# Self-attention in a one-core transformer layer: scores in quarters of the array, the mask written by PE, the maximum read from PSUM

## The reference

```python
def _L0_attn_ref(x, q_heads, k_heads, v_heads, output_proj):
    ...                                   # 16 heads of 16 features
    scores = jnp.einsum('bhqd,bhkd->bhqk', q, k) * scale
    causal = jnp.triu(jnp.ones((S, S), bool), k=1)
    scores = jnp.where(causal, jnp.asarray(-jnp.inf, scores.dtype), scores)
    attn = jax.nn.softmax(scores, axis=-1)
    out = jnp.einsum('bhqk,bhkd->bhqd', attn, v)
    out = out.transpose(0, 2, 1, 3).reshape(B, S, D_MODEL)
    return out @ output_proj.T
x = x + _L0_attn_ref(_layernorm(x, axis=-1), ...)
```

## Time and profile before

| | us |
|---|---|
| median of 3 runs | 1841.96 (1841.55 to 1844.64) |
| profiled execution | 1836.55 |
| its span | 1834.8 |
| `self_attention`: first instruction on POOL to end of the last add | 1349.70 to 1442.76 |
| granted PE clock, mean of the span (1 is 2.4 GHz) | 0.964 |

### The profile page before, as it was taken

How to read it: one execution, slowest core, us unless ns; L and a number is a source line. 1 busy time by engine, 2 the same in 40 slices (tenths; PEclk the granted TensorE clock), 3 DMA queues, 4 the chain that set the end, 5 groups by cost and what they waited for, 6 DMA issues and landing times. The chain is left out here.

```text
span 1834.8 us, 31747 instructions
## 1 busy us (share of the span) xinstructions
PE 1699.0 (93%) x9178; PEld 1392.3 (76%) x9178; DVE 1488.3 (81%) x2950; ACT 1232.4 (67%) x2233; POOL 163.4 (9%) x145
## 2 busy tenths in 40 slices
PE   6599999999999999999999999998978559999994
PEld 4478888888888888888888888874544349999994
DVE  6689999899989998998999899875348558878863
ACT  4577777878777778787787777864324237777761
POOL 0000000000000000000000000000027240000003
PEclk9899999999999999999999999998989769999997
DMA  7722222222222212222223232104830066666732
GB/s 281 283 75 68 73 82 63 73 76 84 70 77 64 87 54 81 72 82 69 80 62 87 58 87 63 36 13 123 301 124 1 2 220 223 225 192 227 222 99 81
DMA packets 171170, 199.02 MB, mean 108 GB/s; under 512 B 19144, under 2 KB 131936, under 8 KB 171104
## 3 DMA queue, kind: packets, MB, share of 16 engines
q1 hardware_dynamic: 169568, 194.00, 33.4%
q0 software_dynamic: 1536, 4.20, 0.7%
HBM read 153.53 MB, written 44.63 MB: 108 GB/s over the span
## 5 line engine op out<-in xcount | busy, mean ns | idle before, releaser
L757 ACT ACTIVATE s<-score,rnow 128x512 f32<-128x512 f32 (+1 forms) x416 | 286.7, 689 | 256.3 <-PE score L143 251.8
L141 PE MATMUL score<-qsh,tl 128*128 128x512 f32 (+1 forms) x832 | 331.7, 399 | 18.7 <-DVE qsl L816 16.4
L142 PE MATMUL score<-qsl,th 128*128 128x512 f32 (+1 forms) x832 | 326.1, 392 | 0.0
L143 PE MATMUL score<-qsh,th 128*128 128x512 f32 (+1 forms) x832 | 325.9, 392 | 0.0
L141 PE MATMUL acc<-ph,cl 128*128 128x512 f32 (+1 forms) x832 | 324.8, 390 | 0.8 <-DVE pl L795 0.7
L142 PE MATMUL acc<-pl,ch 128*128 128x512 f32 (+1 forms) x832 | 324.4, 390 | 0.0
L143 PE MATMUL acc<-ph,ch 128*128 128x512 f32 (+1 forms) x832 | 324.4, 390 | 0.0
L789 DVE TENSOR_TENSOR s<-s,misc 128x512 f32<-128x512 f32 (+1 forms) x416 | 281.7, 677 | 9.1 <-PE misc L720 7.6
L795 DVE TENSOR_TENSOR pl<-s,ph 128x512 fp32r<-128x512 f32 (+1 forms) x416 | 283.7, 682 | 1.6 <-ACT ph L738 1.6
L738 ACT ACTIVATE ph<-s 128x512 fp32r<-128x512 f32 (+1 forms) x416 | 259.1, 623 | 2.2 <-PE acc L143 1.8
L743 ACT ACTIVATE s<-s 128x512 f32<-128x512 f32 (+1 forms) x416 | 258.4, 621 | 2.1 <-DVE s L789 2.1
(11 more groups left out here) (248 smaller groups left out, 2825.4 us busy)
## 6 DMA issues: line engine op xcount, KB each, us to landing
raw<-in_ctx_in SPq DMA_DIRECT2D x192, 128.0 KB, 2.0
turned<-in_turned_in SPq DMA_DIRECT2D x48, 512.0 KB, 3.7
wr<-in_W SPq DMA_DIRECT2D x45, 512.0 KB
queries_scratch<-stage SPq DMA_DIRECT2D x32, 512.0 KB, 3.9
qr<-queries_scratch SPq DMA_DIRECT2D x64, 256.0 KB, 3.6
outputs_scratch<-o SPq DMA_DIRECT2D x64, 256.0 KB, 2.9
at<-outputs_scratch SPq DMA_DIRECT2D x16, 1024.0 KB, 7.7
wr<-in_Wg SPq DMA_DIRECT2D x15, 1024.0 KB
```

The costliest lines, as they stand in the source:

```text
L141: pe.matmul(out, wl, mh, start=first, stop=False, **more)
L142: pe.matmul(out, wh, ml, start=False, stop=False, **more)
L143: return pe.matmul(out, wh, mh, start=False, stop=last, **more)
L757: act.activation(s[0:n, u, t, :], score[0:n, slot(0, u, t) % 2, :], ACT.Copy, scale=rnow[0:n, t:t + 1]).then_inc(copied, 1)
```

## The change

- **Keys.** `mine` now has four columns, one for each fourth head, and `kb` holds each key four times instead of eight, for all 16 sequences at once. VectorE lays the lower half `m` = 0 in one operation for eight sequences, straight from PSUM; ScalarE lays `m` = 1 in four scaled copies. POOL lays none, `kT` is gone, and no keys are laid in the loop. queries_keys(0) and (1) are two parts, with values(0), values(1) and scores(0) between them.
- **Scores.** The mask is cast to fp32r in `above_r`, and PE writes it first into the two banks with two matmuls by the identity `ident_r`. Then come eight matmuls, 64 deep, into 64 partitions by 256 columns (four heads by 64 keys), each with its rows and its output partitions in one of the four quarters of the array, added onto the mask. `above_r` repeats the mask for each head.
- **Maximum and subtraction** read the two PSUM banks directly, and the mask additions on VectorE are gone. The heads now stand in `s` in another order, which `outputs` follows.
- **Values** are made for two sequences at a time, and copied 64x256 at a time.
- **Order.** In the loop PE has scores(i+2), turn(i-1), project(i-2), outputs(i-1); VectorE has invert(i), add(i-3), shift(i+2); ScalarE does exp(i+3) between the copies to `aT` and to `oT`. `turn(0)` waits for all values.
- **POOL** makes the masks first, then a `nil` of 512 columns, then the power for the layer norm; the memset of `vb` waits for the last `ln_xn`. SP clears `XG` with three DMAs that read `nil` repeatedly.

The diff, cut (the removed lines are in the kernel above):

```diff
+        above_r, ident_r = sb("s_above_r", [P, 2 * SG, NQ], F32R), sb("s_ident_r", [P, P], F32R)
+        kb = sb("s_kb", [P, DC, B, SG, NQ], F32)
...
+        nil = sb("s_nil", [P, 2 * DIM], F32)
...
+        vbank = lambda i: 2 + i if i < 2 else 4 + (i - 2) % 4
...
+                for n in range(3):
+                    sp.dma_start(flat[:, n * pieces // 3:(n + 1) * pieces // 3, :],
+                                 nil[:, :].unsqueeze(1).broadcast_to([P, pieces // 3, 2 * DIM])).then_inc(cleared, 16)
+                sp.wait_ge(cleared, 48)
...
             @block.gpsimd
             def _(pool):
-                pool.memset(nil[:, :], 0.0).then_inc(nil_set, 1)
-                pool.memset(mine[:, :], 1.0).then_inc(g1, 1)
...
-                pool.memset(vb[:, :, :, :], 0.0).then_inc(v_zero, 1)
...
+                pool.tensor_tensor(mine[:, :], mine8[:, 0:SG], mine8[:, SG:2 * SG], ALU.add).then_inc(g3, 1)
+                pool.memset(nil[:, :], 0.0).then_inc(nil_set, 1)
                 ln.pool_root(pool)
-                pool.wait_ge(g2, 4)
-
-                def lay_keys(i):
...
-                def normalise(i):
+                pool.wait_ge(ln.norm, TT)
+                pool.memset(vb[:, :, :, :], 0.0).then_inc(v_zero, 1)
+                for i in range(TT):
                     pool.wait_ge(inverted, i + 1)
                     pool.tensor_tensor(s[:, i % 4], s[:, i % 4], inv[:, i % 2, :].unsqueeze(2).broadcast_to([P, SH, NQ]),
                                        ALU.mult).then_inc(normed, 1)
...
+                def queries_keys(t):
                     pe.wait_ge(ln.copied, 2 * t + 2)
...
+                    for m in range(DC):
+                        for kind in range(2):
+                            if t > 0 and kind == 0:
...
+                            if t > 0 and kind == 1:
...
+                            for c in range(DC):
+                                mm = pe.matmul(bank[:, 4 + 2 * m + kind, :], w[:, kind, c, m * P:(m + 1) * P],
+                                               ln.hT[:, c, t * HALF:(t + 1) * HALF], start=c == 0, stop=c == DC - 1)
+                            mm.then_inc(k_made if kind else q_made, 1)
+
+                def values(i):
...
+                    for b2 in range(2):
+                        tokens = side(2 * i + b2)
...
+                            for hh in range(2):
+                                heads = w[:, 2, c, :].rearrange("p (j e d) -> p j e d", e=2, d=SD)[:, :, hh, :]
+                                mm = pe.matmul(bank[side(hh), vbank(i), b2 * P:(b2 + 1) * P], ln.hT[:, c, tokens],
+                                               heads, start=c == 0, stop=c == DC - 1)
                     mm.then_inc(v_made, 1)
 
                 def scores(i):
...
-                    for n in range(4):
...
-                        pe.matmul(bank[b2 * NQ:(b2 + 1) * NQ, 2 * (i % 2) + m, :], qT[:, m, b * NQ:(b + 1) * NQ],
-                                  kb[:, (4 * i + n) % 16, :, :], start=True, stop=True).then_inc(scored, 1)
+                    if i in (0, TT // 2):
...
+                    if i == 0:
+                        pe.wait_ge(cast, 3)
+                    if i == 1:
+                        pe.wait_ge(v_laid, 4)
+                    if i >= 2:
+                        pe.wait_ge(shifted, i - 1)
+                    for r in range(2):
+                        pe.matmul(bank[:, 2 * (i % 2) + r, :], ident_r[:, :], above_r[:, :, :], start=True, stop=True)
+                    for m in range(DC):
+                        for b2 in range(2):
+                            b = 2 * i + b2
+                            for r in range(2):
+                                mm = pe.matmul(bank[side(b2), 2 * (i % 2) + r, m * SG * NQ:(m + 1) * SG * NQ],
+                                               qT[side(r), m, side(b)], kb[side(r), m, b, :, :],
+                                               start=False, stop=True, skip_group_check=True)
+                    mm.then_inc(scored, 1)
...
-                    for pr in range(SPAIRS):
-                        m, r = pr // 4, 32 * (pr % 4)
+                    for m in range(DC):
                         for b2 in range(2):
-                            mm = pe.matmul(bank[r:r + 32, 6, m * P + b2 * NQ:m * P + (b2 + 1) * NQ],
...
+                            for at in range(4):
+                                mm = pe.matmul(bank[32 * at:32 * at + 32, 6, m * P + b2 * NQ:m * P + (b2 + 1) * NQ],
+                                               vb[:, 2 * i + b2, 4 * m + at, :],
+                                               aT[:, i % 2, 4 * (at // 2) + 2 * m + at % 2, b2 * NQ:(b2 + 1) * NQ],
...
-                for i in range(3):
...
-                    scores(i)
...
+                queries_keys(0)
+                values(0)
+                values(1)
+                scores(0)
+                queries_keys(1)
+                scores(1)
+                values(2)
+                values(3)
+                scores(2)
+                for i in range(4, TT):
+                    values(i)
                 pe.wait_ge(wo_in, 16)
-                for i in range(TT):
-                    turn(i)
-                    if i >= 1:
-                        project(i - 1)
-                    if i + 3 < TT:
-                        scores(i + 3)
-                    outputs(i)
+                for i in range(1, TT + 1):
+                    if i + 2 < TT:
+                        scores(i + 2)
+                    turn(i - 1)
+                    if i >= 2:
+                        project(i - 2)
+                    outputs(i - 1)
                 project(TT - 1)
 
...
+                def lay(t):
...
+                        act.wait_ge(q_made, DC * t + m + 1)
+                        act.activation(qT[:, m, t * HALF:(t + 1) * HALF], bank[:, 4 + 2 * m, :], ACT.Copy
+                                       ).then_inc(q_copied, 1)
+                        if t == 1 and m == 0:
+                            exp(0)
...
+                    for f in range(SG):
+                        act.activation(kb[:, 1, t * B // 2:(t + 1) * B // 2, f, :],
+                                       bank[:, 7, :].rearrange("p (b k) -> p b k", k=NQ), ACT.Copy,
+                                       scale=mine[:, f:f + 1]).then_inc(k_laid, 1)
...
+                act.wait_ge(g2, 4)
+                for r, a in enumerate((above, above2)):
+                    act.activation(above_r[side(r), :, :], a[side(r), :].unsqueeze(1).broadcast_to([NQ, 2 * SG, NQ]),
+                                   ACT.Copy).then_inc(cast, 1)
+                act.activation(ident_r[:, :], ident[:, :], ACT.Copy).then_inc(cast, 1)
+                ln.scalar_copy(act)
+                def lay_values(i):
+                    act.wait_ge(v_made, i + 1)
+                    for hh in range(2):
+                        src = bank[side(hh), vbank(i), 0:2 * P].rearrange("p (b j d) -> p b j d", b=2, d=SD)
+                        act.activation(vb[side(hh), 2 * i:2 * i + 2, :, hh * SD:(hh + 1) * SD], src, ACT.Copy
+                                       ).then_inc(v_laid, 1)
+
+                lay(0)
+                act.wait_ge(v_zero, 1)
+                lay_values(0)
+                lay_values(1)
+                lay(1)
+                lay_values(2)
+                lay_values(3)
                 exp(1)
+                for i in range(4, TT):
+                    lay_values(i)
+                exp(2)
                 for i in range(TT):
...
+                    if i + 3 < TT:
+                        exp(i + 3)
...
-                    if i + 2 < TT:
-                        exp(i + 2)
 
             @block.vector
             def _(v):
...
-                v.wait_ge(g2, 4)
...
+                def lay_keys(t):
+
+                    v.wait_ge(k_made, DC * t + 1)
+                    keys = bank[:, 5, :].rearrange("p (b k) -> p b k", k=NQ)
+                    v.tensor_tensor(kb[:, 0, t * B // 2:(t + 1) * B // 2, :, :],
+                                    keys.unsqueeze(2).broadcast_to([P, B // 2, SG, NQ]),
+                                    mine[:, :].unsqueeze(1).unsqueeze(3).broadcast_to([P, B // 2, SG, NQ]),
                                     ALU.mult).then_inc(k_laid0, 1)
 
                 def shift(i):
...
-                    for m in range(2):
...
-                        v.tensor_tensor(s[:, i % 4, 8 * m:8 * m + 8, :], bank[:, 2 * (i % 2) + m, :],
-                                        above[:, :].unsqueeze(1).broadcast_to([P, 8, NQ]), ALU.add).then_inc(masked, 1)
...
+                    both = bank[:, 2 * (i % 2):2 * (i % 2) + 2, :].rearrange("p r (h k) -> p (r h) k", k=NQ)
...
+                    v.tensor_reduce(top[:, i % 2], both, AX_X, ALU.max).then_inc(topped, 1)
...
+                    if i >= 4:
+                        v.wait_ge(turned, 2 * (i - 3))
+                    v.tensor_tensor(s[:, i % 4], both, top[:, i % 2].unsqueeze(2).broadcast_to([P, SH, NQ]),
```

(80 more changed lines are left out.)

105 lines of the change are left out of this document (25 added, 80 removed).

## The result

The change makes the kernel faster: median 1818.55 us (4 runs, 1814.61 to 1818.62) against 1843.3 for the kernel before on the same chip (4 runs), ratio 0.9865 with a 95% interval of 0.9842 to 0.9888. In a second series it is 1818.24 (6 runs) against 1840.37 (10 runs), 0.9884 (0.9862 to 0.9907). The forecast was 1818.3. Against the kernel before on the same chip the saving is 24.75 us, where 23.7 was forecast; the forecast started from the 1841.96 of the first three of these four runs, so part of the closeness of the two totals is chance.

A forecast was written before the change was run, and what follows sets the result against it. VectorE, busy 9.86 of 10 us, was taken as the bound. Savings of 2.5 at the head, 13.4 in the loop and 7.8 in filling and emptying make 23.7: 1841.96 - 23.7 = 1818.3 us, range 1811 to 1830.

The forecast's parts named there:

- filling: Stage start up to the first reciprocal, forecast at 1383.45; filling and emptying the pipeline together were to save 7.8 us.
- tail: From the last reciprocal, forecast at 1410.85, to the stage's last add at 1419.05.
- VectorE's tile: Steady loop: without mask adds and keys (2.76), VectorE's 6.93 us a tile falls to 4.22.
- The bound from below: VectorE's PSUM reads: perhaps 0.1 us less, the subtraction sharing one SBUF input less with POOL; 0.05 more was taken.
- PE's round: Steady loop on PE: scores 1.50, turn 0.93, project 0.96, outputs 0.74 and 0.1 make 4.23 us a tile.
- Pace: Steady loop: PE and VectorE level at 4.25 us a tile instead of 6.93, 13.4 saved over five tiles.
- Head: Stage start: POOL's memset of `vb` moved back lets `xn` start 2.54 us earlier; 2.5 saved.
- (a): Score products: quarters run only two at a time, scores 0.86 us longer, +6.9, total 1825.2; chance 0.14.
- (b): Score products: quarters run one after the other, +2.58 us a tile, +20.6, total 1838.9; chance 0.04.
- (c): Score products: small matmuls do not overlap their own load and way out, +70 us, total 1888; chance 0.02.
- (d): PE's clock falls for the whole loop, 3.4 us of streaming a tile doubles, +27, total 1845; chance 0.04.
- (e): Start goes faster than reckoned (clock up sooner, keys and values cheaper), 2 to 4 us more, 1815; chance 0.08.

The follow-up runs named there:

- a_no_mask: Changed kernel without the two mask matmuls of each tile on PE; steady tile 4.08 us, stage 66.20, total 1820.03 us (1 run).
- the three kernels on the pace: Changed kernel without mask matmuls, with maximum and row sum over half the keys, or with both: steady tile 4.08, 4.16 and 3.50 us.
- a_memset_free: Changed kernel without the wait that keeps POOL's memset of `vb` behind the last `ln_xn`; stage 72.09 us, total 1821.0 us (1 run).
- b_head: Kernel before with only POOL's order at the stage's start changed, as in the change; median 1843.18 us, ratio to before 1.0007.
- a_old_order: Changed kernel with the loop orders of PE, ScalarE and VectorE all put back; median 1824.9 us, ratio to before 0.9902.
- a_pe_order: Changed kernel with PE's loop order alone put back; median 1833.16 us, ratio to before 0.9948.

## Why the prediction was right

The mechanism was right: VectorE was the bound, the work taken off it turned into time, and PE and VectorE came out level. The near agreement of the stage, 69.4 forecast and 69.26 measured, is partly luck: the filling was 0.65 longer than reckoned, the loop 0.2 and the tail 0.5 shorter, and in PE's round, too, errors of both signs cancel.

- **VectorE's tile**, forecast 4.22. Its work is 4.08 (a_no_mask), so the reads from PSUM cost nothing: maximum 1.22 and subtraction 1.22, against 1.22 and 1.31 in SBUF. The bound from below, that the subtraction has one SBUF input less to share with POOL, was the right side, as the subtraction from PSUM takes the 1.22 that it takes in SBUF with POOL idle.
- **PE's round**, forecast 4.23, measured 4.16, and the sum hides errors of both signs. Scores were put at 1.50 and take 0.67 + 1.02 = 1.69. The products alone would be 0.86, so the steps at their ends are some 0.16; masks are 0.67 where 0.46 was reckoned, so theirs are some 0.2. I had taken 0.09 for each, from the step up to the first half-array matmul on the earlier trace rows. The same rows show that the next step is long too, 22.10 - 21.77 = 0.33 instead of 0.23: with it a change of shape costs 0.19, and I had read half of it. Against that, outputs takes 0.58, not 0.74, and the 0.1 put on top of the round was not needed. Full overlap of four quarters was right: in the single records of the trace four start within 0.02 us and the next four 0.22 later.
- **The Trainium skill's two points.** TensorEngine Tiling (Array Packing), Key Properties, has the mode change drain the array: the trace agrees in so far as masks and products each cost 0.16 to 0.2 us more than their streaming. By TensorE: Matmul & The Clock Gate, Measured speedup vs the span model, the products would have been an estimated 1.12 instead of 0.86. Measured are 1.02 with the steps in it, so its 3.07x for four row tiles does not carry over to these four quarters.
- **Pace**, forecast 4.25, measured 4.16, over the loop 27.19 against 1410.85 - 1383.45 = 27.4. "PE and VectorE are level" is what the three kernels on the pace show.
- **Head**, forecast 2.5, measured 2.55 (7.76 - 5.21). What it is worth at the end of the new stage no run shows directly. a_memset_free comes nearest: of 3.15 lost at `ln_xn` 2.83 arrive at the first reciprocal and at the end, so that chain passes on nine tenths. Done alone on the kernel before, the head brings 1.6 of 2.5 in the stage, which the expectation of b_head had not foreseen.
- **Filling**, first reciprocal 33.7 after the start, measured 34.36. This step was 0.6 too short, and all of that is there at scores(0): its masks start 20.4 after the stage instead of 19.9 (ScalarE's keys 0.2 later, 2.42 instead of 2.3, and 0.26 from them to PE where 0.1 was taken), and the result takes 1.80 instead of 1.6, for the masks as above.
- **Tail**, forecast 8.2, measured 7.71: turn(7) starts 3.08 after the last reciprocal (1415.93 - 1412.85) instead of 3.35, and from there to the end of the copy to `oT` it is 3.00 instead of 3.2, outputs again.
- **Rivals.** (a) does not happen, but its price is right (6.9 forecast and built). (b) and (c) are excluded by 1.02 us for sixteen records. (d): the clock stood at 1.00 from 1375 to 1416. (e): the start was not quicker.
- **What the order is worth** stood in the prediction only as a wait that "does not come back". It is 5.7 of the 23.8, by a_old_order. That an order on one engine has to fit those of the others (14.4 lost when it does not) the prediction did not say.
- **What no run separates**: no kernel puts the mask additions or the keys back on VectorE, so that their 2.76 a tile is read from the rows of before, and none gives the kernel before the new orders alone.

## What to carry to other kernels

Count the bound engine's work and the next one's before taking work away: here most of the gain (18.1 of 23.8 us) was there with the loop's old orders too, and with the new ones it ended where PE became level. Orders on different engines are changed together or not at all: all three new ones brought 5.7, while the old one on PE beside the new ones on the others cost 14.4. Matmuls with a shallow contraction and few output partitions are worth packing by quarters of the array, with some 0.2 us to be reckoned for each change of shape. A memset on POOL belongs where VectorE has no SBUF-only work on the way, and a gain at the start of a pipeline counts only after a look at what its loop does when it comes earlier.

## What the runs showed of the hardware

- Four 64x64 quarters run fully side by side, whatever the order of issue: sixteen fp32 records of 256 columns in 1.02 to 1.04 us, against 1.93 when only the column halves can.
- A change of tile shape between PE matmuls costs 0.16 to 0.2 us here: masks and products take that much more than their streaming, and on the earlier trace rows two steps in a row are long, by 0.09 and 0.10.
- VectorE's maximum and subtraction over 1024 fp32 columns take 1.22 us from PSUM as from SBUF. With both inputs in SBUF and keys being laid on POOL, the subtraction took 1.30, 1.85 and 2.03 when the POOL operation under way had 0.22, 0.77 and 0.95 left (b_head), and the next POOL operation took 2.02 instead of 1.04.
- The eight `ln_xn` took 3.15 us longer beside a POOL memset of 3.51, and an operation of eight elements a row waited it out (2.06 instead of 0.17), though the memset reads nothing. The first of the eight took 3.57, to 0.15 after the memset's end; the others took their usual time.
- In b_head the granted clock fell from 1.00 to 0.50 within two microseconds after one without any PE record (2.26 us from record to record), and stayed at 1.00 after a gap of 2.25 us two tiles later. In a_pe_order it fell in the first tiles and stayed at 1.00 through gaps of 2.8 us in the steady ones.
